# A fused S4D, linear and gated-LoRA block on one core: the first weight turned by TensorE instead of by DMA, with a new prologue, stores by head and a last product in two column halves

## What is computed

```python
# x: (32 c, 128 h, 64 n, 2); everything is float32
h = s4d_kernel(log_dt, C=x, B, inv_A_real, A_imag, L=1024)   # (c, h, l): 2*Re sum_n Cc * exp(dtA*l)
h = h + einsum('bsi,oi->bso', layernorm(h), attn_weight) + attn_bias        # weight 1024 x 1024
y = layernorm(h)
base = einsum('bsi,oi->bso', y, W) + b                                      # weight 1024 x 1024
gates = softmax(einsum('bsi,ei->bse', y, Wr))                               # E = 4
proj = einsum('bsi,eri->bser', y, A)                                        # R = 8
h = h + base + einsum('bse,bseo->bso', gates * 2, einsum('bser,eor->bseo', proj, Bm))
```

## Time and profile before

| | us |
|---|---|
| median of 3 runs | 875.21 (874.69 to 875.56) |
| the profiled execution, its own time | 874.79 |
| its span in the profile | 873.0 |
| TensorE matmuls busy | 791.8 (91%) |
| VectorE busy | 587.1 (67%) |
| ScalarE busy | 337.3 (39%) |

### The profile page before, as it was taken

One profiled execution on the slowest core, in us unless ns is written; L12 is line 12 of the kernel. 1 busy time (PEld: TensorE's weight loads), 2 busy tenths in 40 slices (PEclk: granted clock), 3 DMA queues, 4 the chain that ended last, 5 costly groups with the idle time before them and its releaser, 6 DMA issues.

```text
span 873.0 us, 15563 instructions
## 1 busy us (share of the span) xinstructions
PE 791.8 (91%) x6082; PEld 405.5 (46%) x6082; DVE 587.1 (67%) x1077; ACT 337.3 (39%) x561; POOL 70.1 (8%) x40
## 2 busy tenths in 40 slices
PE   0346599999999999999999999999999999999994
PEld 0323254544455454545455454545455454555442
DVE  7797857576877667576867667675767677675430
ACT  5886424242524243342524243342525242342210
POOL 0012002020201002020202001020202010000000
PEclk9967899999999999999999999999999999999998
DMA  7796923333234233333333223333333323333321
GB/s 288 194 172 122 170 51 73 68 76 72 60 72 84 52 73 73 63 77 69 64 74 79 63 66 73 64 77 66 74 74 68 72 62 70 68 63 69 68 49 48
DMA packets 189993, 72.48 MB, mean 83 GB/s; under 512 B 175348, under 2 KB 183668, under 8 KB 189976
## 3 DMA queue, kind: packets, MB, share of 16 engines
q1 hardware_dynamic: 189976, 72.27, 38.3%
HBM read 13.52 MB, written 16.78 MB: 35 GB/s over the span
## 4 chain that ended last, share of the span: by engine, by line
PE 58%; DVE 16%; issue 13%; ACT 9%; SPq 1%; DMA 1%; POOL 1%; DVEq 0%; ACTq 0%; POOLq 0%
PE ps_g L432 27%; PE ps_g L408 20%; PE ps_a L397 6%; DVE h_tok L931 2%; DVE y L917 2%; ACT junk L577 2%; ACT L564 2%; DVE h_tok L892 2%; DVE m_im L883 2%; PE ps_g L443 2%; ACT turn_u L564 2%; ACT x_tok L591 2%; DVE stat L903 1%; DVE params L773 1%; SPq L315 1%
## 5 line engine op out<-in xcount | busy, mean ns | idle before, releaser
L408 PE MATMUL ps_g<-wa_hi,x 128*128 128x512 f16 x1024 | 272.7, 383 | 11.0 <-DVE h_tok L931 6.0
L432 PE MATMUL ps_g<-wf_hi,x 128*128 128x512 f16 x1024 | 274.2, 382 | 8.2 <-DMA wf_lo<-stage 7.5
L408 PEld LDWEIGHTS ps_g<-wa_hi,x 128*128 128x128 f16 x1024 | 98.0, 98 | 133.2 <-issue 16.2
L408 PE MATMUL ps_g<-wa_lo,x 128*128 128x512 f16 x512 | 154.9, 382 | 0.0
L432 PEld LDWEIGHTS ps_g<-wf_hi,x 128*128 128x128 f16 x1024 | 98.7, 99 | 117.5 <-issue 9.8
L432 PE MATMUL ps_g<-wf_lo,x 128*128 128x512 f16 x512 | 153.3, 381 | 0.0
L571 ACT ACTIVATE junk<-ps_a,stat 128x1024 bf16<-128x1024 f32 x32 | 35.6, 1112 | 142.0 <-DVE stat L895 142.0
L989 DVE SCALAR_TENSOR_TENSOR result<-ps_g,unscale,h_tok 128x1024 f32<-128x1024 f32 x32 | 41.1, 1284 | 72.2 <-PE ps_g L443 72.2
L740 POOL TENSOR_TENSOR phase<-z_turn,steps_b 128x1024 f32<-128x1024 f32 x15 | 39.0, 2598 | 573.8 <-DVE turn_u L862 559.6
L397 PE MATMUL ps_a<-turn_u,m 128*32 128x128 f32 x2048 | 65.9, 283 | 20.1 <-DVE m L886 15.3
L408 PEld LDWEIGHTS ps_g<-wa_lo,x 128*128 128x128 f16 x512 | 50.4, 98 | 61.3 <-issue 1.9
(11 more groups left out here) (157 smaller groups left out, 817.3 us busy)
## 6 DMA issues: line engine op xcount, KB each, us to landing
out<-result SPq DMA_DIRECT2D x32, 512.0 KB
x_raw<-in_x SPq DMA_DIRECT2D x64, 64.0 KB
stage<-in_L_ffn_W SPq DMA_DIRECT2D x8, 512.0 KB, 15.3
h_tok<-in_L_attn_weight SPq DMA_DIRECT2D x2, 512.0 KB, 5.5
x<-in_L_attn_weight SPq DMA_DIRECT2D x2, 512.0 KB, 7.8
result<-in_L_attn_weight SPq DMA_DIRECT2D x2, 512.0 KB, 9.2
x<-x_tok SPq DMA_TRANSPOSE x64, 3.2
x<-stage SPq DMA_TRANSPOSE x64, 3.2
```

Of the source, the lines that this page charges most:

```text
L408: mm = pe.matmul(ps_g1[:, o, :], x1_part(part)[:, k, :], ws[:, k, o * HALF:(o + 1) * HALF], start=k == 0 and part == 0 and ws is wa_hi, st ...
L432: pe.matmul(ps_g2[:, o, :], xs[:, k, :], ws[:, k, o * HALF:(o + 1) * HALF], start=k == 0 and xs is x2_hi and ws is wf_hi, stop=False)
```

## The change

- **First weight.** It is no longer split by rows and turned by DMA. TensorE turns each raw float32 block with eight transposes of 128x128 into free PSUM (`turn_weight`); ScalarE and VectorE split it from PSUM straight into `wa_hi` and `wa_lo` (`attn_hi`, `attn_lo`). The blocks use `ps_g2`, `ps_g1`, `ps_g2`, `ps_g1`, (block 6) `ps_x` with `ps_p`, (block 5) `ps_a`, and `ps_g2` again for blocks 4 and 7, each after the reader before has let go. The 16 DMA transposes of `wa` are gone; those of `wf` stay.
- **Loads.** The 8 blocks of the first weight are issued by ScalarE's own queue as its first instructions, beside the small inputs and x on SyncE's. The second weight's loads wait for block 4 of the first.
- **Prologue order.** The first waves are made in halves of 4 heads; `s4(0, 1)`, `attn(0, 0)`, the row sums and the second weight's split are reordered on all engines; `s4(1, 0)` moves from ahead of `attn(0, 1)` into the first second-layer product, behind its 24th matmul.
- **Stores.** Each store of a half is four DMAs, one for each head (32 rows of 4 KB), instead of one.
- **End.** The last second-layer product, of half (15, 1), goes to `ps_g1` by column halves: 24 matmuls and one LoRA matmul, then the same for the other 512 columns. Each half is finished and stored by itself; the last four stores are issued two by SyncE and two by ScalarE.

```diff
@@ block.sync
-            turn_weights(0, 3)
             turn_x1(0, 0)
-            turn_weights(3, KB)
+            sp.wait_ge(s_wt, KB)
+            sp.wait_ge(s_wsum, KB)
             sp.dma_start(wg_rows[0:ER, :], lora_a.rearrange("e r i -> (e r) i")).then_inc(s_wg, 16)
             sp.dma_start(wg_rows[ER:G, :], gate_w).then_inc(s_wg, 16)
+            turn_x1(0, 1)
             load_x(2)
-            turn_x1(0, 1)
-            sp.wait_ge(s_wa[0], 128)
-            sp.wait_ge(s_wa[1], 128)
-            turn_weights(KB, KB + 5)
+            turn_weights(KB, 2 * KB)
             turn_x2(0, 0)
-            turn_weights(KB + 5, 2 * KB)
             turn_x1(1, 0)
             turn_x2(0, 1)
...
@@ block.tensor
+            def turn_weight(n):
+                pe.wait_ge(s_wload[n], 16)
+                for ps, ks in attn_pieces(n):
+                    for k in range(ks.start, ks.stop):
+                        mm = pe.transpose(ps[:, (k - ks.start) * P:(k - ks.start + 1) * P],
+                                          raw_block(n)[:, k * P:(k + 1) * P], ident[:, :])
+                mm.then_inc(s_wt, 1)
...
+            pe.wait_ge(s_q, 2)
+            turn_weight(0)
+            turn_weight(1)
             s4(0, 0)
+            pe.wait_ge(s_wlo, 1)
+            turn_weight(2)
+            pe.wait_ge(s_wlo, 2)
+            turn_weight(3)
+            pe.wait_ge(s_xt_sb, 1)
+            pe.wait_ge(s_pre_act, 3)
+            turn_weight(6)
+            pe.wait_ge(s_xn1, 1)
+            turn_weight(5)
+            pe.wait_ge(s_wlo, 3)
+            turn_weight(4)
+
+            pe.wait_ge(s_x1, 32)
+            pe.wait_ge(s_wlo, 4)
+            attn_part(0, 0, range(0, 4), (0,))
+            pe.wait_ge(s_wlo, 5)
+            turn_weight(7)
+            attn_part(0, 0, range(4, KB), (0,))
+            pe.wait_ge(s_wlo, 6)
+            s4(0, 1)
+            pe.wait_ge(s_wlo, KB)
+            attn_part(0, 0, range(KB), (1,)).then_inc(s_g1, 1)
...
-            s4(1, 0)
-            attn(0, 1)
             pe.wait_ge(s_wg_hi, 1)
             pe.wait_ge(s_wg_lo, 1)
             project(0, 0)
             pe.wait_ge(s_lb_sb, 2)
             pe.wait_ge(s_wf, 32 * KB)
-            ffn_part(0, 0, range(0, 6))
+            ffn_part(0, 0, range(0, 4))
+            s4(1, 0)
+            ffn_part(0, 0, range(4, 6))
             turn_lora(0, 0)
             ffn_part(0, 0, range(6, KB))
             ffn_end(0, 0)
...
@@ block.scalar
+            for n in range(KB):
+                act.dma_start(raw_block(n), attn_rows[n]).then_inc(s_wload[n], 16)
             act.preload_act_table_set("exp_and_others")
+            act.wait_ge(s_fill, 1)
+            row_sum(0, 0)
...
-            row_sum(4, 4)
+            for n in range(1, 4):
+                row_sum(n, n)
...
             sines(0)
-            for n in range(5, KB):
+            for n in range(4, KB):
                 row_sum(n, n)
...
-            weight_hi(0, 4)
+            attn_hi(0)
             square_1(0, 0, KB)
             rstd_guess(0, 0, stat_1, s_ssq1, s_log1, s_y1)
-            weight_hi(4, 5)
+            attn_hi(1)
             high_1(0, 0)
-            weight_hi(5, KB)
-            copy_x(1)
+            attn_hi(2)
+            attn_hi(3)
+            attn_hi(4)
+            attn_hi(5)
+            first_decays(1)
+            attn_hi(6)
+            attn_hi(7)
...
@@ block.vector
-            weight_lo(0, 2)
             keep_h(0, 0)
-            weight_lo(2, 3)
+            attn_lo(0)
             normalise_1(0, 0)
-            weight_lo(3, 4)
+            attn_lo(1)
             low_1(0, 0)
+            for n in range(2, 6):
+                attn_lo(n)
+            make_first_u(1)
             make_m(0, 1)
-            weight_lo(4, 6)
-
+            for n in range(6, KB):
+                attn_lo(n)
             keep_h(0, 1)
-            weight_lo(6, KB)
-            round_turns(1)
             normalise_1(0, 1)
-            make_m(1, 0)
             low_1(0, 1)
-            make_u(1)
-            split_lora_b()
+            keep_h2(0, 0)
             weight_top(1, f_sum, 2 * KB + 1)
             split_scales(1)
+            normalise_2(0, 0)
+            ffn_lo(KB, 2 * KB)
+            low_2(0, 0)
+            round_turns(1)
+            split_lora_b()
...
```

More of the change, by code:

```diff
@@ L301, in load_x @@
                         sp.dma_start(x_raw[:, i, twice, :], x_rows[columns(T, i), :, :]).then_inc(s_x, 16)
[L303 to L307, removed]
             def turn_weights(first, end):
                 for n in range(first, end):
-                    landed = s_wa[n // 4] if n < KB else s_wf
                     for part, ready in enumerate((s_whi, s_wlo)):
                         sp.wait_ge(ready, n + 1)
-                        sp.dma_start_transpose(weight_block(n, part), split_block(n, part)).then_inc(landed, 16)
+                        sp.dma_start_transpose(turned_block(n, part), split_block(n, part)).then_inc(s_wf, 16)
             def turn_x1(t, i):
@@ L370, in _ @@
                     turn_x2(t, i)
[L371 to L374, removed]
+            t = TILES - 1
+            store(t, 0)
+            for o in range(2):
+                sp.wait_ge(s_result_last, o + 1)
+                for q in range(HS if o == 0 else 2):
+                    sp.dma_start(out_rows[HT * t + HS + q, :, o * HALF:(o + 1) * HALF],
+                                 result[q * C:(q + 1) * C, 1, o * HALF:(o + 1) * HALF]).then_inc(s_out[1], 16)
+            sp.wait_ge(s_out[0], 64 * TILES)
+            sp.wait_ge(s_out[1], 64 * (TILES - 1) + 128)
         @block.tensor
@@ L399, in s4, with attn_part @@
                 mm.then_inc(s_s4, 1)
[L401 to L405, removed]
+            def attn_part(t, i, ks, halves=(0, 1)):
+                for k in ks:
                     for part, ws in ((0, wa_hi), (0, wa_lo), (1, wa_hi)):
@@ L410, in attn @@
                                            stop=k == KB - 1 and part == 1)
-                if 1 in halves:
-                    mm.then_inc(s_g1, 1)
+                return mm
+            def attn(t, i):
+                pe.wait_ge(s_x1, 32 * (2 * t + i + 1))
+                at_least(pe, s_h2, 2 * t + i)
+                attn_part(t, i, range(KB)).then_inc(s_g1, 1)
+            def turn_weight(n):
[5 more added lines that the diff above has]
+                mm.then_inc(s_wt, 1)
             def project(t, i):
@@ L521, in _ @@
             project(t, 1)
[L522 to L525, removed]
+            pe.wait_ge(s_h2, 2 * TILES)
+            for o in range(2):
+                cols = slice(o * HALF, (o + 1) * HALF)
+                for k in range(KB):
+                    if (o, k) == (0, 6):
+                        turn_lora(t, 1)
+                    for part, ws in ((0, wf_hi), (0, wf_lo), (1, wf_hi)):
+                        pe.matmul(ps_g1[:, o, :], x2_part(1, part)[:, k, :], ws[:, k, cols],
+                                  start=k == 0 and part == 0 and ws is wf_hi, stop=False)
+                pe.wait_ge(s_lora_sb, 2 * TILES)
+                pe.matmul(ps_g1[:, o, :], lora_t[:, :], lb[:, cols], start=False, stop=True).then_inc(s_g2_last, 1)
         @block.scalar
@@ L543, in first_phases, with first_decays @@
                 a.then_inc(s_quarter, 1)
-            def first_decays():
-                act.wait_ge(s_pre_act, 3)
-                for k in range(HT):
+            def first_decays(half):
+                for k in range(HS * half, HS * half + HS):
                     a = act.activation(decay[:, k, :], steps_b[:, :], ACT.Exp, scale=z_re[:, k:k + 1])
-                a.then_inc(s_decay, 1)
+                a.then_inc((s_decay_0, s_decay)[half], 1)
             def quarters(T):
@@ L644, in _ @@
             first_phases()
-            for n in range(4):
-                row_sum(n, n)
+            copy_x(0)
             act.wait_ge(s_bias, 16)
@@ L687, in _ @@
                            scale=scale[:, 1:2]).then_inc(s_wg_hi, 1)
+            quarters(1)
+            decays(1)
             for o in range(2):
@@ L725, in _ @@
             gate_exp(t, 1)
+            act.wait_ge(s_result_last, 2)
+            for q in range(2, HS):
+                act.dma_start(out_rows[HT * t + HS + q, :, HALF:L], result[q * C:(q + 1) * C, 1, HALF:L])\
+                    .then_inc(s_out[1], 16)
         @block.gpsimd
@@ L1074, in _ @@
                                      op0=ALU.mult, op1=ALU.subtract).then_inc(s_wg_lo, 1)
+            make_m(1, 0)
+            make_u(1)
             keep_h(1, 0)
```

121 lines of the change are left out of this document (75 added, 46 removed).

## The result

| | before | after |
|---|---|---|
| median | 874.95 (874.41 to 875.56, 4 runs) | 884.53 (882.37 to 885.66, 4 runs) |
| span of the profiled execution, its own time | 873.0, 874.79 | 883.4, 885.22 |

The ratio is 1.0106, with an interval of 1.0092 to 1.0119: 9.6 us slower, where 6.4 were forecast (881.6, range 877 to 887). The spans differ by 10.4 us, because the profiled execution after was one of the longer of its four.

The account below looks back on a forecast made before the run. TensorE sets the steady time, so only the ends could change: +15.0 at the first, -8.6 at the second, +6.4 in all. From 874.79 that gives 881.2, plus 0.42 for the median: 881.6 us, range 877 to 887.

Parts of the forecast that it names:

- The first end: Everything up to the end of the first second-layer product: it would end at 135.2 against 120.2, 15.0 us lost.
- the walk: Prologue in the new order, summed with durations from the old profile: product start at 102.8, 104.2 with allowances.
- at 7 us or later: Sign of being wrong: a small chain on VectorE that begins at 7 us or later.
- The steady part: Steady loop: a store issued as four DMAs, costed at nothing; 1.6 us on each of 32 halves if uncovered.
- TensorE idles 12.8 us: At turn_lora(0, 0) in the first second-layer product: TensorE waits for VectorE's chain, 15.35 + 0.07 - 2.6 = 12.8 us.
- 0.8 for the small inputs: Start of the prologue: four small inputs share DMA engines with the first weight; 0.8 us late, bounds nothing to 5 us.
- Rival (b): Prologue: the small inputs come 3 to 5 us late, and everything behind them; 884 to 888; chance 0.15.
- (a): Whole kernel: the forecast as summed holds, with its own range 878.5 to 885; chance 0.66.
- 104.2: Start of the first second-layer product, at 104.2 us, 2.1 us earlier than before.
- 31.0 us from the product's start: First second-layer product with moved s4(1, 0), stall and LoRA pair: 31.0 us, where 13.9 were before.
- The clock, by a page: Prologue: if transposes do not count for the clock gate, about 2 us more; kept in the range.
- The second end: Last product and stores: product ends at 860.3, last store lands by 864.4; 8.6 us won.

Follow-up runs that it names:

- e4: The kernel before with the changed end alone: stores by head, last product in column halves, last four stores from two queues; 866.33 us, ratio 0.9898.
- e1: The changed kernel with s4(1, 0) taken out of the first second-layer product and put ahead of project(0, 0); 877.36 us, ratio 1.0030.
- e6: The changed kernel with the edits of e1 and e2 together; 871.10 us, ratio 0.9958 to the kernel before.
- e8: e2 with VectorE's chain for tile 1 moved between the second weight's splits and s4(1, 0) put behind attn(0, 1); 864.53 us, ratio 0.9880.
- e2: The changed kernel, but ScalarE waits for the four small inputs before issuing the first weight's loads; 880.01 us, ratio 1.0056.
- e7: The changed kernel with small inputs issued by ScalarE ahead of the weights on one queue, and x held until they landed; 879.86 us, ratio 1.0055.
- e9: e2 with GpSimd's second wave (decay of tile 1) held until the coefficients m of (0, 1) are made; 876.91 us, ratio 1.0029.
- e3: The changed kernel with the four small inputs issued from ScalarE's queue ahead of the weights, SyncE beginning with x; 882.70 us, ratio 1.0081.
- e5: The kernel before with stores by head alone; 868.00 us, ratio 0.9917.

## Why the prediction came out right

The first end was put at 15.0 us lost and took 19.6; the second at 8.6 us won and gave 9.2. The mechanism that makes the kernel slower, the stall behind the moved `s4(1, 0)`, was right, and its size too (12.8 forecast, 12.79 measured). That the number came so near was in part luck. 7.3 us of errors in the walk were met by 3.3 us of errors the other way, 2.0 of them from a clock that no run explains: with the product as I had summed it, the median would have been 886.5, half a microsecond inside the range. And the profiled execution lies 0.7 us above its median, where I had put it 0.4 below, which takes 1.1 us more off the miss.

Of the signs that I had written down, the stall, its release by the last step of `gate_end`, the matmuls going on from 135 us, and the short end with a DMA share near 1 came true. The product's start near 104 did not. And one sign of being wrong came true: VectorE's small chain began at 9.2 us, where I had written "at 7 us or later".

- **The steady part:** nothing, as said; e4 shows it alone.
- **"TensorE idles 12.8 us" at the LoRA transpose:** 12.79. Both counts, 15.35 us for VectorE's chain and 12 matmuls that run beside it, were borne out. The stall is 12.79 or 12.80 in all five kernels that keep the order. And e1, e6 and e8 show that the place of `s4(1, 0)` together with VectorE's order makes the stall.
- **"0.8 for the small inputs":** here the size was wrong. They came 4.9 us late, 4.1 more than I took, near the upper bound of 5. I chose near the lower end because they are issued in the first 2 us; but e2 and e7 show that an early issue doesn't help beside bulk loads of another queue. Rival (b)'s event, which I had given 0.15, came about on top of the forecast's, and its 884 to 888 held the time as well as the 878.5 to 885 of (a).
- **"104.2", the product's start:** 110.8. 4.1 of the 6.6 are the small inputs. The walk also took 3.6 us for `make_m(0, 1)` and 1.95 for `s4(0, 1)`; they took 1.7 and 1.5 more, since GpSimd's wave fell beside VectorE's step (e9); the walk has no term for that. The rest of the walk, with its allowance for error, came out 0.7 us shorter.
- **"31.0 us from the product's start":** 29.0. The 24 matmuls took 6.9 us and not 8.0, the 12 behind the stall 3.9 and not 5.0: the clock rose sooner than in the earlier trace rows. No run tells why. Behind the same stall the same 12 matmuls took from 3.85 (e7) to 5.12 us (e2, e3, e9), so my 5.0 was a fair price and the 3.88 a lucky draw; the 24 took 6.42 to 6.87.
- **The clock, by a page:** the 16 transposes of 50.12 to 54 us ran at a granted 0.50, which is 1.2 GHz. From 54.00 to 56.53 TensorE did nothing but float32 transposes. Through 54.00 to 56.70 the granted clock was 0.62 on the mean, which makes some 0.65 us at full clock, and behind it 1.00: it rose near 56.05, during transposes. The Trainium skill, "TensorE: Matmul & The Clock Gate", Part 4, says of TensorE's transpose mode that it does not count; for these transposes (the profile does not name their mode) the trace disagrees, so the 2 us that it would have cost were not lost.
- **The second end:** 3.6 us lie behind the last matmul, where 4.1 were in my sum (860.3 to 864.4). The last stores were issued when I took it, ScalarE's two from 880.58 to 881.43, behind a matmul that ended at 879.77; but they landed in 1.7 and 1.9 us, not 2.3. Ahead of the last matmul the new end saved 0.9 us in e4, where I took 0.8. The Trainium skill, "DMA: Bandwidth & Descriptors", "Why a DMA increments its semaphore by 16 and not by 1", gives the engine count that I used. The traces agree as far as they go: a share of 0.99 in e5 with at most three stores out, where one old store had 0.24.

Sum: +19.6 - 9.2 = +10.4, 4.0 over the forecast's 6.4: 4.1 for the small inputs, 3.2 for the collision and its clock, less 0.7 in the rest of the walk, 2.0 in the product and 0.6 at the end.

## What to carry to other kernels

Removing work ahead of a fixed bound (here sixteen DMA transposes, one every 1.37 us) gives only what the bound itself moves, while each call that is moved to make room drags its successors along: ask which engine waits for the last of them. A small load that starts an engine's chain should land before bulk loads of another queue begin; that costs one wait and gave 4.5 us. A last store whose outermost count is 4 is worth splitting by that count: it gave 7.3 us by the medians. In the middle of the loop, which hides the stores, the split neither cost nor gave anything.

## What the runs showed that I had not expected

- A 64 KB load took 2.0 us with only x behind it on its own queue, 2.6 with eight 512 KB loads behind it there, 4.4 with those behind it and x on the other queue, and 7.0 with the eight on the other queue.
- VectorE's product of two SBUF tiles, 128x1024, took 2.92 us beside GpSimd's product and 1.22 without it; GpSimd's took 2.81 and 1.90. The Trainium skill, "GPSIMD Engine Reference", "1. Specifications", names this contention, for VectorE instructions with two SBUF inputs, without a price. The trace agrees. The times of e2 fit engines that take turns, as an estimate from its rows: the wave began 1.06 us before VectorE's first product ended and took 0.91 longer, and the second product began 1.83 us before the wave ended and took 1.70 longer. No run tests this further.
- 1.7 us more of idle time ahead of `s4(0, 1)` cost another 1.7 us through the lower clock (e2 against e9, a granted 0.50 against 1.00).
